# Moving additions of expert rows, and one stream's normed rows, from VectorE to GpSimd

## The chip, the cores and the metric

The kernel runs on one core of a Trainium2 chip. The metric is the time of one execution on the device in microseconds (us), the median over several runs.

## The reference

A residual x of 32 x 128 tokens with 128 features goes through four layers, each of an attention against a context of the same size and a layer of experts. In short:

```python
x = x + memory_hops(context, layernorm(x))        # first attention, two hops
x = x + top2_experts(layernorm(x))                # 8 experts, 512 hidden, gelu
x = x + linear_attention(layernorm(x), context)   # second attention, 16 heads of 8
x = x + top2_experts_gated(layernorm(x))          # 8 experts, 256 hidden
x = x + latent_attention(context, layernorm(x))   # third attention, 16 heads of 64
x = x + top2_experts_silu(layernorm(x))           # 8 experts, 256 hidden
x = x + masked_attention(layernorm(x), context)   # fourth attention, one head
x = x + top1_expert(layernorm(x))                 # 8 experts, 512 hidden
```

With two experts for a token, each expert writes its weighted output rows, and the two rows of a token are added to x at the start of the attention that follows.

## The kernel before, in words

**Layout.** x stays in SBUF as `X` (`x_rows`): 32 tiles of 128 tokens by 128 features. Four tiles are a group (`G = 4`), so there are eight groups. The second and the fourth attention run in two turns (`TURNS = 2`) of four streams (`W = 4`): group g = 4 i + w is stream w of turn i. Each stream has two PSUM banks. TensorE weaves the streams: it turns the normed rows of streams 0 to 3 (L665), then makes the queries of each, and so on.

**Expert rows.** The experts' stage before wrote two rows for each token into DRAM by indirect DMAs that GpSimd issues (L1539). `load_pairs` brings them back (SyncE, L1709): eight loads of 512 KB, the first four at once, each of the others when the same stream's load of turn 0 has landed (`pairs_here[w]`). The tile in the rows below is `paired_rows`. `combine_stream` waits for `pairs_here[w]`, and `combine` adds the two rows of a group's tokens to x in two TENSOR_TENSORs of 128 x 512 on VectorE (L566). The second attention does it for the first layer's experts, the fourth for the third layer's. In both, `next_rows` adds and then makes the statistics of a stream (`known`: L480, L476). The groups of turn 0 come first. In the second attention groups 4 to 7 are then fitted in between steps of turn 0: group 4 before the maxima, 5 before the read of the attention's output, 6 before the read of the projection, 7 after the tail's norms. In the fourth, groups 4 and 5 come right after the head's norms, 6 and 7 after the maxima.

**Norms.** `norm_rows` is used for the head of a turn (rows that go into the attention) and for its tail (rows that go to the next experts). ScalarE makes the scales by a logarithm and an exponential, `refine_scales` refines them in one step of three VectorE instructions (L449 to L451), and then four TENSOR_SCALARs of 128 x 128 for each stream subtract the mean and multiply by the scale (L498); both scalars are columns in SBUF. Each stream signals TensorE when its four are done. In the fourth attention the tail of turn 1 is made in two halves by functions of its own. There `placed_together` (L2773, L2774), behind the head's norms of turn 1, reads counts from the bank of stream 3, and TensorE turns stream 3 into that bank only after it. In the second attention L1801 adds the projection (L1859) to x; in the fourth L2746 makes the maxima of the scores (L2638), and L2755 reads the mixed rows (L2646).

**GpSimd.** It has no instructions in the second attention. In the fourth it fills a padding tile (a memset, a drain, a cast at L2606), and later sends rows to DRAM by indirect DMAs. The third attention begins on GpSimd with `norm_context`: a copy (L2058), a drain, a subtraction (L2060), a drain, a product (L2062). In the routing stages GpSimd issues indirect DMAs at L745 and L2120, in the experts' stages at L1530 and L1539. A `drain` lets what is behind it on its engine start when what is ahead of it is done.

Of the kernel before, what the change touches and what calls it, by code (L numbers as in the profile page):

```python
# [13 lines left out]
ALU = mybir.AluOpType  # L14
# [9 lines left out]
P = 128  # L24
B = 32
G = 4
NG = B // G
# [92 lines left out]
def build(nc, A, out):  # L120
    with ExitStack() as top:
# [122 lines left out]
        pairs_combined = counter("pairs_combined")  # L244
        latents_normed = counter("latents_normed")
# [200 lines left out]
        def refine_scales(ch, dve, rstd, work):  # L446
# [4 lines left out]
            ch.link(dve.scalar_tensor_tensor(rstd, sq, 1.5, rstd, ALU.add, ALU.mult))  # L451

        def scales_by_log(ch, dve, i, tail, var, rstd, work, begun=False):
# [4 lines left out]
            refine_scales(ch, dve, rstd, work)  # L458
# [29 lines left out]
        def norm_rows(dve, ch, i, tail, st, src, dst, signal, free=None, begun=False):  # L488

            if not begun:  # L490
                ch.link()
            scales_by_log(ch, dve, i, tail, st["mv"][:, :, 1], st["rstd"][:, :], st["work"], begun)
# [9 lines left out]
        def head_norms(dve, ch, i, SS, st, T, begun=False):  # L502
# [3 lines left out]
                      lambda w: dve.wait_ge(SS[w].act.sem, turn_before(SS[w].ACT, i)), begun)  # L506
# [79 lines left out]
        def tail_norms(dve, ch, i, SS, st, T, taken=False, src=x_tile):  # L586
# [5 lines left out]
            for w in range(W):  # L592
                aggregate_stream(dve, st, w)
            norm_rows(dve, ch, i, 1, st, lambda w: src(i * W + w), lambda w: tile_in(T[w]["tl"]["rows"]),
                      lambda w, ins: ins.then_inc(SS[w].dve.sem, SS[w].DVE.tick("tail_normed")))
# [1115 lines left out]
        def close_rows(layer):  # L1711
            for c in pairs_here:
                c.value += 16 * TURNS

# [18 lines left out]
        def attention_1(layer_before):  # L1733
            assert layer_before in SCATTERED
            with ExitStack() as ph:
# [28 lines left out]

                @block.vector
                def _(dve):
# [40 lines left out]
                    for i in range(TURNS):  # L1807
                        if i == 0:
                            head_norms(dve, ch, i, SS, st, T)
# [4 lines left out]
                        tail_norms(dve, ch, i, SS, st_tail, T, taken=True)  # L1814
                        for _ in ahead:
                            pass
                        if i < TURNS - 1:
                            begin_scales(dve, ch, st)
                            keep_logits(dve, i, SS, T)
                            head_norms(dve, ch, i + 1, SS, st, T, True)  # L1820
# [69 lines left out]
                close_streams(SS)  # L1890
                close_rows(layer_before)
# [667 lines left out]
        def attention_3(layer_before):  # L2559
            SCALE = float(P) ** -0.5  # L2560
            with ExitStack() as ph:
# [165 lines left out]
                def _(dve):  # L2727
# [76 lines left out]
                    for i in range(TURNS):  # L2804
                        if i == 0:
                            head_norms(dve, ch, i, SS, st, T)
# [4 lines left out]
                        if i < TURNS - 1:  # L2811
                            tail_norms(dve, ch, i, SS, st_tail, T, src=last_x)
# [4 lines left out]
                            head_norms(dve, ch, i + 1, SS, st, T, True)  # L2817
# [50 lines left out]
```

## Time and profile before

| what | us |
|---|---|
| median of 3 runs | 1673.55 (1666.23 to 1673.93) |
| the profiled execution | 1664.46 |
| its span | 1662.6 |
| second attention, about | 357 to 440 |
| fourth attention, about | 1438 to 1520 |

The span is the time from the first to the last instruction of the profiled execution; its time is 1.9 us more. TensorE's granted clock was 0.897 of full speed in the mean. In the rows, PE is TensorE, DVE VectorE, ACT ScalarE, POOL GpSimd and SPq SyncE's queue; L566 is line 566 of the kernel before. A bracket behind a row is the idle time of the engine before it and what ended it; "issue" means that the profile shows no releaser.

### The profile page before, as it was taken

The numbers are of one execution on the slowest core, as the hardware profiler recorded it, in microseconds if no ns is written. First come the engines' busy times: TensorE is split into PE (matmuls) and PEld (weight loads), VectorE is DVE, ScalarE is ACT, GpSimd is POOL, SyncE is SP. The second block draws the span as 40 slices with busy tenths as digits, with TensorE's granted clock in tenths as the row PEclk, the third lists the DMA queues.
The fourth block names the chain that finished last, engine by engine and source line by source line (L and its number), as shares of the span: only waits on it lengthen the run. The fifth ranks groups of instructions, "written<-read, shape, count | busy, mean of one in ns | idle before, by whom it ended". The sixth has DMA issues, their size and how long they took to land. (4 is left out here: it accounts for less than half of the span.)

```text
span 1662.6 us, 37562 instructions
## 1 busy us (share of the span) xinstructions
PE 1398.9 (84%) x10866; PEld 1301.8 (78%) x10867; DVE 1121.4 (67%) x3528; ACT 903.6 (54%) x2726; POOL 767.3 (46%) x775
## 2 busy tenths in 40 slices
PE   6687699946877389999999999999998399667398
PEld 4566599945666289999999999999998399545298
DVE  5646755558767367778787877878776466576455
ACT  4354155522323178777778787777775134244254
POOL 4066444420004454556757575757554456303344
PEclk9797899977657699999999999999999699878599
DMA  9201122250220300000000000000000323531322
GB/s 233 34 32 57 52 57 67 64 182 1 103 75 30 123 14 1 14 2 19 10 16 10 7 19 0 25 0 13 1 14 6 107 79 84 164 103 52 115 81 70
DMA packets 88412, 88.70 MB, mean 53 GB/s; under 512 B 17058, under 2 KB 74761, under 8 KB 87927
## 3 DMA queue, kind: packets, MB, share of 16 engines
q1 hardware_dynamic: 72472, 58.20, 12.8%
q0 software_dynamic: 12448, 26.27, 4.6%
q10 hardware_dynamic: 3392, 3.02, 0.7%
q8 instruction: 47, 0.77, 0.2%
q14 instruction: 53, 0.43, 0.1%
HBM read 54.06 MB, written 34.91 MB: 54 GB/s over the span
## 5 line engine op out<-in xcount | busy, mean ns | idle before, releaser
L2130 POOL TENSOR_TENSOR paired_rows<-paired_rows,rinv 128x1024 f32<-128x1024 f32 x128 | 242.7, 1896 | 243.6 <-DVE rinv L2451 228.6
L2442 DVE TENSOR_TENSOR probs_turned_lo<-psum_banks,probs_turned_hi 128x512 fp32r<-128x512 f32 x256 | 175.5, 686 | 137.7 <-ACT probs_turned_hi L2295 133.3
L2321 ACT ACTIVATE paired_rows<-psum_banks,neg_max 128x256 f32<-128x256 f32 x512 | 237.2, 485 | 0.6 <-DVEq L2022 0.4
L2242 PE MATMUL psum_banks<-probs_turned_hi,y_rows 128*128 128x256 f32 x1024 | 214.8, 293 | 0.9 <-DVEq L2022 0.9
L2192 PE MATMUL psum_banks<-y_turned_parts,queries_hi 128*128 128x256 f32 x1024 | 199.6, 293 | 3.0 <-DVEq L2022 3.0
L2242 PEld LDWEIGHTS psum_banks<-probs_turned_hi,y_rows 128*128 128x128 f32 x1024 | 167.5, 190 | 1.7 <-DVEq L2022 1.6
L2295 ACT CAST probs_turned_hi<-psum_banks 128x512 fp32r<-128x512 f32 x256 | 151.2, 591 | 19.9 <-PE psum_banks L2163 8.3
L2192 PEld LDWEIGHTS psum_banks<-y_turned_parts,queries_hi 128*128 128x128 f32 x1024 | 157.7, 190 | 3.6 <-issue 3.6
L2163 PE MATMUL psum_banks<-ident,paired_rows 128*128 128x128 f32 x1024 | 155.5, 274 | 5.3 <-DVE probs_turned_lo L2442 2.9
L2457 DVE TENSOR_REDUCE neg_max<-psum_banks 128x4 f32<-128x1024 f32 x128 | 155.4, 1214 | 3.7 <-PE psum_banks L2192 3.5
L2192 PE MATMUL psum_banks<-y_turned_parts,queries_lo 128*128 128x256 f32 x512 | 145.0, 283 | 0.0
L2242 PE MATMUL psum_banks<-probs_turned_lo,y_rows 128*128 128x256 f32 x512 | 144.5, 282 | 0.0
L2295 ACT CAST queries_hi<-psum_banks 128x512 fp32r<-128x512 f32 x128 | 75.0, 586 | 106.0 <-PE psum_banks L2228 97.6
L2163 PEld LDWEIGHTS psum_banks<-ident,paired_rows 128*128 128x128 f32 x1024 | 116.7, 140 | 8.7 <-DVE probs_turned_lo L2442 3.6
L1601 ACT ACTIVATE hidden<-psum_banks,tile_w 128x128 f32<-128x128 f32 x284 | 81.4, 368 | 65.4 <-PE psum_banks L1564 51.2
L1539 POOL DMA_INDIRECT expert_rows<-expert_rows_sb,tile_rows x71 | 68.1, 959 | 97.1 <-DVE expert_rows_sb L1648 94.8
L2321 ACT ACTIVATION_READ_ACCUMULATOR paired_rows<-psum_banks,neg_max 128x1 f32 x512 | 110.2, 215 | 0.0
L2228 PE MATMUL psum_banks<-y_turned_parts,wqk_hi 128*128 128x256 f32 x512 | 103.8, 295 | 0.8 <-POOL y_turned_parts L2054 0.8
L2242 PEld LDWEIGHTS psum_banks<-probs_turned_lo,y_rows 128*128 128x128 f32 x512 | 97.7, 191 | 0.0
L2192 PEld LDWEIGHTS psum_banks<-y_turned_parts,queries_lo 128*128 128x128 f32 x512 | 97.1, 190 | 0.0
L745 POOL DMA_INDIRECT rows_by_expert_first<-paired_rows,top_experts x64 | 62.5, 976 | 70.7 <-DVE mix_weights L1126 49.3
L1539 POOL DMA_INDIRECT expert_rows<-expert_rows_sb__,tile_rows x71 | 68.2, 960 | 58.1 <-ACT expert_rows_sb__ L1608 57.4
(721 smaller groups left out, 3787.1 us busy)
## 6 DMA issues: line engine op xcount, KB each, us to landing
paired_rows<-expert_rows SPq DMA_DIRECT2D x16, 512.0 KB, 6.0
expert_w_a<-rows_by_expert_last SPq DMA_DIRECT2D x39, 129.0 KB
tile_rows<-rows_by_expert_first SPq DMA_DIRECT2D x71, 65.0 KB
tile_rows<-rows_by_expert SPq DMA_DIRECT2D x71, 65.0 KB
expert_w_b<-in_L_ffn_w_dram SPq DMA_DIRECT2D x2, 2048.0 KB, 12.6
tile_rows<-expert_rows SPq DMA_DIRECT2D x8, 512.0 KB, 3.7
x_rows<-in_x_dram SPq DMA_DIRECT2D x8, 256.0 KB, 5.4
ctx_turned_dram<-ctx_turned SPq DMA_DIRECT2D x1, 2048.0 KB, 11.1
```

What stands on the lines that cost most here:

```text
L745: pool.indirect_dma_start(xfirst, bass.IndirectOffsetOnAxis(ap=first_spots[:, i, k, t:t + 1], axis=0), ROWS[:, i * N + t, :], None).then_i ...
L1539: pool.indirect_dma_start(ys, bass.IndirectOffsetOnAxis(ap=to, axis=0), yo[:, i % SLOTS, :], None).then_inc(expert_out[i % SLOTS].sem, 16)
L1601: ins = act.activation(hidT[:, s % 2, c * P:(c + 1) * P], hidden_bank(s, c // 2)[:, c % 2 * P:(c % 2 + 1) * P], ACT.Gelu, bias=w1[:, s % 4 ...
L2130: ins = pool.tensor_tensor(probs[:, k, :, :], probs[:, k, :, :], rinv[:, k, :].unsqueeze(2).to_broadcast([P, 4, 256]), ALU.mult)
L2163: ins = pe.transpose(bank[T_BANK][:, h * P:(h + 1) * P], probs[:, par, h, c * P:(c + 1) * P], ident[:, :])
L2192: ins = pe.matmul(bank[S_BANKS[par] + r][:, h * 256:(h + 1) * 256], queries[q][:, h, r, :], yparts[:, 2 * s2 + y, r * 256:(r + 1) * 256], ...
L2228: ins = pe.matmul(bank[Q_BANK][:, h * 256:(h + 1) * 256].rearrange("p (r q) -> p r q", r=2), wqk_parts[w][:, 2 * u3 + h, :], latents_of, s ...
L2242: ins = pe.matmul(bank[Z_BANK][:, r * 256:(r + 1) * 256], yrows[:, 2 * s1 + y, (2 * r + k) * P:(2 * r + k + 1) * P], probsT[x][:, (u + 1) ...
L2295: ins = act.copy(dst, bank[bank_][:, :])
L2321: ins = act.activation(probs[:, par, h, :], bank[S_BANKS[par] + h // 2][:, (h % 2) * 256:(h % 2 + 1) * 256], ACT.Exp, bias=nmax[:, par, h: ...
L2442: ins = dve.tensor_tensor(lo, bank[bank_][:, :], hi.bitcast(F32), ALU.subtract)
L2457: ins = dve.tensor_reduce(nmax[:, par, :], ps[:, S_BANKS[par]:S_BANKS[par] + 2, :].rearrange("p r (h k) -> p (r h) k", k=256), AX.X, ALU.m ...
```

## The change

In the second and the fourth attention GpSimd makes the additions of groups 2 to 7 (six of eight), with a drain between the two additions of a group, and VectorE waits for a count (`pairs_added`) instead of adding. And GpSimd makes the normed rows of stream 3: a subtraction and a product of 128 x 512 with the mean and the scale broadcast, and a drain between them, after VectorE has refined the scales (`scales_refined`, raised by the last instruction of `refine_scales`). That goes for the four norms of the second attention and for the first three of the fourth; the fourth's last tail stays as it was. GpSimd's order is: additions of groups 2 and 3, head norm, additions of groups 4 to 7, tail norm, head norm (and in the second attention a tail norm). In the fourth this stands behind the padding tile and ahead of the indirect DMAs. Cut to its core:

```diff
+        def last_stream_norm(pool, n, st, src, dst, signal, free=None):
+            own = slice((W - 1) * G, W * G)
+            pool.wait_ge(scales_refined.sem, scales_refined.value + n)
+            if free:
+                free()
+            pool.tensor_tensor(dst, src, st["mv"][:, own, 0:1].to_broadcast([P, G, P]), ALU.subtract)
+            pool.drain()
+            pool.tensor_tensor(dst, dst, st["rstd"][:, own].unsqueeze(2).to_broadcast([P, G, P]), ALU.mult).then_inc(signal, 1)
...
+        POOL_GROUPS = [g for g in range(NG) if g >= W // 2]
+
         def combine_stream(dve, ch, i, w, layer):
 
+            g = i * W + w
+            if g in POOL_GROUPS:
+                dve.wait_ge(pairs_added.sem, pairs_added.value + POOL_GROUPS.index(g) + 1)
+                return
             dve.wait_ge(pairs_here[w].sem, i * 16 + (pairs_here[w].value + 16))
-            combine(dve, ch, i * W + w, layer)
+            combine(dve, ch, g, layer)
+
+        def combine_on_pool(pool, layer, i):
+
+            for g in POOL_GROUPS:
+                if g // W != i:
+                    continue
+                w = g % W
+                pool.wait_ge(pairs_here[w].sem, i * 16 + (pairs_here[w].value + 16))
+                for k in range(CHOICES[layer]):
+                    if k:
+                        pool.drain()
+                    ins = pool.tensor_tensor(group(X, g), group(X, g), YY[:, bass.ds(g * G, G), k, :], ALU.add)
+                ins.then_inc(pairs_added.sem, 1)
...
@@ norm_rows
-            for w in range(W):
+            for w in range(W - 1 if by_pool else W):
...
@@ attention_1, a new GpSimd stream
+                @block.gpsimd
+                def _(pool):
+                    combine_on_pool(pool, layer_before, 0)
+                    for i in range(TURNS):
+                        own, S = group(X, i * W + W - 1), SS[W - 1]
+                        last_stream_norm(pool, 2 * i + 1, st, own, T[W - 1]["u"][:, :, :], S.dve.sem, lambda: pool.wait_ge(S.act.sem, turn_before(S.ACT, i)))
+                        if i < TURNS - 1:
+                            combine_on_pool(pool, layer_before, i + 1)
+                        last_stream_norm(pool, 2 * i + 2, st_tail, own, T[W - 1]["tl"]["rows"][:, :, :], S.dve.sem)
...
@@ attention_3, GpSimd, ahead of its spreads
+                    combine_on_pool(pool, layer_before, 0)
+                    S = SS[W - 1]
+                    first, second = ((i * W + W - 1) * G for i in range(TURNS))
+                    last_stream_norm(pool, 1, st, X[:, first:first + G, :], T[W - 1]["u"][:, :, :], S.dve.sem, lambda: pool.wait_ge(S.act.sem, turn_before(S.ACT, 0)))
+                    combine_on_pool(pool, layer_before, 1)
+                    last_stream_norm(pool, 2, st_tail, LAST_ROWS[:, first:first + G, P:2 * P], T[W - 1]["tl"]["rows"][:, :, :], S.dve.sem)
+                    last_stream_norm(pool, 3, st, X[:, second:second + G, :], T[W - 1]["u"][:, :, :], S.dve.sem, lambda: pool.wait_ge(S.act.sem, turn_before(S.ACT, 1)))
```

## Rows read from the trace of the kernel before

**Rows 1.** Page, part 1: busy us of each engine, share of the span, instructions.

```profile
PE 1398.9 (84%) x10866; PEld 1301.8 (78%) x10867; DVE 1121.4 (67%) x3528; ACT 903.6 (54%) x2726; POOL 767.3 (46%) x775
```

**Rows 2.** Timeline, VectorE, second attention: start, duration, line, tiles; in brackets the wait before.

```profile
367.62 1.43 DVE L566 TENSOR_TENSOR x_rows<-x_rows,paired_rows 128x512 f32<-128x512 f32 x2
...
370.47 0.38 DVE L476 BATCH_NORM_AGGREGATE mean_var__<-norm_stats__ 128x2 f32<-128x6 f32 x4
...
375.56 1.11 DVE L498 TENSOR_SCALAR u_rows___<-x_rows,mean_var__,rstd__ 128x128 f32<-128x128 f32 x4
...
403.81 0.69 DVE L1801 TENSOR_TENSOR x_rows<-x_rows,psum_banks 128x512 f32<-128x512 f32 x1 [0.98 <-PE psum_banks L1859]
```

**Rows 3.** Timeline, TensorE, second and fourth attention.

```profile
376.72 1.12 PE L665 MATMUL psum_banks<-ident,u_rows___ 128*128 128x128 f32 x4
...
1476.02 3.82 PE L2646 MATMUL psum_banks<-ctx_rows,expert_w_a 128*128 128x128 f32 x32
...
1508.26 0.63 PE L665 MATMUL psum_banks<-ident,u_rows___ 128*128 128x128 f32 x4 [0.90 <-DVE ends L2774]
```

**Rows 4.** Timeline, VectorE, fourth attention.

```profile
1468.79 0.69 DVE L2746 TENSOR_REDUCE neg_max<-psum_banks 128x4 f32<-128x512 f32 x1 [3.14 <-PE psum_banks L2638]
...
1479.14 1.13 DVE L2755 SCALAR_TENSOR_TENSOR paired_rows<-psum_banks,rinv,x_rows 128x128 f32<-128x128 f32 x4
```

**Rows 5.** Groups by form, VectorE and GpSimd: busy us, mean ns | idle before, releaser.

```profile
L566 DVE TENSOR_TENSOR x_rows<-x_rows,paired_rows 128x512 f32<-128x512 f32 x32 | 21.8, 682 | 12.5 <-DMA paired_rows<-expert_rows 10.9 <-issue 0.5
...
L2071 POOL TENSOR_TENSOR x_rows<-x_rows,paired_rows 128x512 f32 x10 | 12.9, 1295 | 2.6 <-issue 2.6
```

**Rows 6.** Timeline, GpSimd, start of the third and of the fourth attention.

```profile
558.27 0.19 POOL L2058 COPY group_scale<-ctx_rstd 128x4 f32<-128x4 f32 x1 [1.78 <-POOLq L1446]
567.71 1.04 POOL L2060 TENSOR_TENSOR context_normed<-ctx_rows,ctx_mean_var 128x512 f32<-128x512 f32 x1 [9.25 <-issue]
568.91 1.03 POOL L2062 TENSOR_TENSOR context_normed<-context_normed,group_scale 128x512 f32<-128x512 f32 x1 [0.15 <-issue]
...
1446.01 0.36 POOL L2606 CAST last_pad<-spare_row 128x1 uint32<-128x1 f32 x1 [7.26 <-issue]
```

**Rows 7.** Timeline, SyncE's DMA queue, second attention.

```profile
362.37 0.36 SPq L1709 DMA_DIRECT2D paired_rows<-expert_rows  x1
```

**Rows 8.** Page, part 5: GpSimd's indirect DMAs before attention stages.

```profile
L1539 POOL DMA_INDIRECT expert_rows<-expert_rows_sb,tile_rows x71 | 68.1, 959 | 97.1 <-DVE expert_rows_sb L1648 94.8
...
L745 POOL DMA_INDIRECT rows_by_expert_first<-paired_rows,top_experts x64 | 62.5, 976 | 70.7 <-DVE mix_weights L1126 49.3
...
L1539 POOL DMA_INDIRECT expert_rows<-expert_rows_sb__,tile_rows x71 | 68.2, 960 | 58.1 <-ACT expert_rows_sb__ L1608 57.4
```

**Rows 9.** Groups by line, GpSimd, windows 500 to 557 and 1283 to 1311 us.

```profile
L1530 POOL DMA_INDIRECT tile_rows<-normed_rows_dram,source_rows x16 | 16.0, 997 | 28.4 <-SPq L1446 23.9 <-issue 4.3 <-PE psum_banks L1554 0.3
...
L1539 POOL DMA_INDIRECT expert_rows<-expert_rows_sb_,pair_rows x16 | 15.9, 996 | 5.3 <-issue 3.7 <-ACT expert_rows_sb_ L1610 1.0 <-DMA expert_rows<-expert_rows_sb_,pair_rows 0.6
...
L2120 POOL DMA_INDIRECT rows_by_expert<-paired_rows,top_experts x16 | 15.4, 963 | 19.7 <-DVE top_experts L2408 15.4 <-issue 4.3
```

**Rows 10.** Timeline, VectorE and ScalarE, start of the third attention.

```profile
565.81 0.17 DVE L2518 TENSOR_SCALAR rows_work<-rows_mv 128x8 f32<-128x8 f32 x1
...
571.83 0.20 ACT L2279 ACTIVATE rows_work<-rows_work 128x8 f32<-128x8 f32 x1
```

**Rows 11.** Timeline, VectorE and GpSimd side by side; last a group of VectorE.

```profile
348.98 0.52 DVE L1648 TENSOR_SCALAR expert_rows_sb<-expert_rows_sb,tile_rows 128x128 f32<-128x128 f32 x1
...
348.51 0.96 POOL L1539 DMA_INDIRECT expert_rows<-expert_rows_sb,tile_rows  x1 [0.94 <-DVE expert_rows_sb L1648]
...
134.12 1.11 DVE L498 TENSOR_SCALAR u_rows__<-x_rows,mean_var_,rstd_ 128x128 f32<-128x128 f32 x4
...
135.04 0.32 POOL L750 COPY paired_rows<-mix_weights 128x4 f32<-128x4 f32 x1 [5.32 <-ACT u_turned L642]
...
L1648 DVE TENSOR_SCALAR expert_rows_sb<-expert_rows_sb,tile_rows 128x128 f32<-128x128 f32 x71 | 20.3, 286 | 0.1
```

More of the change, by code:

```diff
@@ L244, in build @@
         pairs_combined = counter("pairs_combined")
+        scales_refined = counter("scales_refined")
+        pairs_added = counter("pairs_added")
         latents_normed = counter("latents_normed")
@@ L444, in seed_scales, with refine_scales @@
             ch.link(dve.tensor_scalar(rstd.bitcast(I32), bits, -1.0, RSQRT_SEED, ALU.mult, ALU.add))
-        def refine_scales(ch, dve, rstd, work):
+        def refine_scales(ch, dve, rstd, work, refined=None):
             half, sq = work[:, 0, :], work[:, 1, :]
@@ L450, in refine_scales, with scales_by_log @@
             ch.link(dve.tensor_tensor(sq, sq, half, ALU.mult))
-            ch.link(dve.scalar_tensor_tensor(rstd, sq, 1.5, rstd, ALU.add, ALU.mult))
-        def scales_by_log(ch, dve, i, tail, var, rstd, work, begun=False):
+            ins = dve.scalar_tensor_tensor(rstd, sq, 1.5, rstd, ALU.add, ALU.mult)
+            if refined:
+                ins.then_inc(refined.sem, 1)
+            ch.link(ins)
+        def scales_by_log(ch, dve, i, tail, var, rstd, work, begun=False, refined=None):
             if not begun:
@@ L457, in scales_by_log @@
             dve.wait_ge(roots_made.sem, i * 2 + (roots_made.value + 1 + tail))
-            refine_scales(ch, dve, rstd, work)
+            refine_scales(ch, dve, rstd, work, refined)
         def roots_by_log(act, i, tail, st):
@@ L486, in known, with norm_rows @@
             aggregate_stream(dve, st, w)
-        def norm_rows(dve, ch, i, tail, st, src, dst, signal, free=None, begun=False):
+        def norm_rows(dve, ch, i, tail, st, src, dst, signal, free=None, begun=False, by_pool=None):
             if not begun:
                 ch.link()
-            scales_by_log(ch, dve, i, tail, st["mv"][:, :, 1], st["rstd"][:, :], st["work"], begun)
-            for w in range(W):
+            scales_by_log(ch, dve, i, tail, st["mv"][:, :, 1], st["rstd"][:, :], st["work"], begun, scales_refined if by_pool else None)
+            for w in range(W - 1 if by_pool else W):
                 if free:
@@ L500, in norm_rows, with head_norms @@
                 signal(w, ins)
-        def head_norms(dve, ch, i, SS, st, T, begun=False):
+            if by_pool:
+                by_pool()
+        def last_stream_norm(pool, n, st, src, dst, signal, free=None):
[6 more added lines that the diff above has]
+            pool.tensor_tensor(dst, dst, st["rstd"][:, own].unsqueeze(2).to_broadcast([P, G, P]), ALU.mult).then_inc(signal, 1)
+        def head_norms(dve, ch, i, SS, st, T, begun=False, pooled=False):
             norm_rows(dve, ch, i, 0, st, lambda w: x_tile(i * W + w), lambda w: tile_in(T[w]["u"]),
                       lambda w, ins: ins.then_inc(SS[w].dve.sem, SS[w].DVE.tick("u_normed")),
-                      lambda w: dve.wait_ge(SS[w].act.sem, turn_before(SS[w].ACT, i)), begun)
+                      lambda w: dve.wait_ge(SS[w].act.sem, turn_before(SS[w].ACT, i)), begun,
+                      (lambda: SS[W - 1].DVE.tick("u_normed")) if pooled else None)
         def begin_scales(dve, ch, st):
@@ L584, in tail_tiles, with tail_norms @@
                     "ix": sb_in(ph, "tail_index", [P, G, E], U32), "lg": sb_in(ph, "tail_logits", [P, G, E])}
-        def tail_norms(dve, ch, i, SS, st, T, taken=False, src=x_tile):
+        def tail_norms(dve, ch, i, SS, st, T, taken=False, src=x_tile, pooled=False):
             if not taken:
@@ L594, in tail_norms @@
             norm_rows(dve, ch, i, 1, st, lambda w: src(i * W + w), lambda w: tile_in(T[w]["tl"]["rows"]),
-                      lambda w, ins: ins.then_inc(SS[w].dve.sem, SS[w].DVE.tick("tail_normed")))
+                      lambda w, ins: ins.then_inc(SS[w].dve.sem, SS[w].DVE.tick("tail_normed")),
+                      by_pool=(lambda: SS[W - 1].DVE.tick("tail_normed")) if pooled else None)
         def tail_dve(dve, ch, g, i, S, tl, logits_bank, hot=None, to=ROWS.bitcast(U32)[:, :, P]):
@@ L1713, in close_rows @@
                 c.value += 16 * TURNS
+            pairs_added.value += len(POOL_GROUPS)
         def load_expert_weights(sp, layer):
@@ L1813, in _ @@
                         ch.link()
-                        tail_norms(dve, ch, i, SS, st_tail, T, taken=True)
+                        tail_norms(dve, ch, i, SS, st_tail, T, taken=True, pooled=True)
                         for _ in ahead:
@@ L1890, in attention_1 @@
                 close_streams(SS)
+                scales_refined.value += 2 * TURNS
                 close_rows(layer_before)
@@ L2805, in _ @@
                         if i == 0:
[L2806 removed]
+                            head_norms(dve, ch, i, SS, st, T, pooled=True)
                         ahead = next_rows(dve, ch, i + 1, st, here, (2, 2))
```

8 lines of the change are left out of this document (4 added, 4 removed).

## The prediction

> **What bounds the kernel now.** I read the page's totals first [rows 1]. TensorE is busy for 84% of the span, VectorE for 67% and GpSimd for 46%, so over the whole kernel VectorE isn't the limit, and GpSimd has room. But the change touches two stages, the second attention (357 to 440 us) and the fourth (1438 to 1520 us), and there the order of VectorE's work has to be read from its timeline. The reader should look at two things in it: what ends a wait, and what would be late next if VectorE were done sooner.
>
> At the start of the second attention [rows 2] each group has its additions and then its statistics, and the last of these end at 370.85. The refined scales are there at 372.40, and 16 TENSOR_SCALARs (four for each stream, one each 0.257 us) give the normed rows of streams 0 to 3 at 373.59, 374.61, 375.64 and 376.67. TensorE turns the last of these at 376.72 for 1.12 us [rows 3]: a turn takes it as long as VectorE needs for a stream, so what makes stream 2 late makes everything after it as late. Later additions are mostly put in front of waits: at 403.81 VectorE had waited 0.98 us for TensorE, at 1468.79 it had waited 3.14 us [rows 2, 4]. The groups of additions that start at once are the costly ones: of 21.8 us in 32 additions only those that start a stage, or stand ahead of something that is ready, are on the path [rows 5].
>
> **The change, part by part.** *Additions taken from VectorE.* 24 of 32 additions go, 24 x 0.682 = 16.4 us [rows 5], and 28 TENSOR_SCALARs of 0.257 = 7.2 us. If all of it lay on the path the kernel would gain 23.6 us; that is one bound. In the second attention the additions of group 4 stand behind the head's norms (0.68 us each, ahead of the waits for TensorE's first products), the others ahead of waits as that at 403.81 [rows 2]. I take -0.1. In the fourth all four groups of turn 1 stand between the maxima and the mixed rows. There TensorE's mixed products of the first stream (32 products in 3.82 us, that is four streams, 0.96 each) start at 1476.02, and VectorE reads them at 1479.14 [rows 3, 4]. Ready they were at about 1477.2 (0.96 and some 0.2 until the wait is passed): -1.9.
>
> *Additions put on GpSimd.* The same shape takes it 1.295 us [rows 5], with 0.15 us between two instructions that a drain parts [rows 6], so 2.75 us for a group. The pairs of group 2 land at 362.37, when SyncE's queue passes its wait for them and issues the seventh load [rows 7]. Without anything else groups 2 and 3 would have their rows at 362.5 + 2 x 2.75 + 0.15 = 368.1, against VectorE's 369.05 (367.62 + 1.43) [rows 2]; as VectorE has the statistics of group 2 to make in between, I count -0.65.
>
> *The drain between the two additions.* This is the term with the widest bounds. Nothing in the kernel before drains GpSimd in the second attention. Where it does drain, the trace has two kinds of gap [rows 6]. After compute alone it is 0.15 us. After a stretch of indirect DMAs it is 7.26 us in the fourth attention, between a memset and the cast at 1446.01, and 9.25 us at the start of the third, between a copy and the subtraction at 567.71, and the profile names no releaser ("issue"). The indirect DMAs since the last drain are 71 + 16 = 87 in the one case, and 64 + 71 + 16 + 16 = 167 in the other [rows 8, 9]. 7.1 / 87 = 0.082 us for each; 9.1 / 167 = 0.054, so it grows with their number, or to a limit. At the second attention 64 + 71 = 135 wait. Bounds: 7.3 us (the nearest smaller count) and 11 us (135 x 0.082), and below nothing, -0.65, if the drain's gap belongs to something else. I take 9.1. Group 2: first addition 362.5 to 363.8, drain to 372.9, second to 374.2; group 3 at 374.2 + 2.75 + 0.15 = 377.1, seen by VectorE at about 377.2. Statistics and aggregates of that stream ended 370.85, 1.8 us after its additions (369.05) [rows 2]: now 379.0. **+8.1.** VectorE stands in the wait for group 2 with everything behind it, and TensorE has nothing until the first stream is normed.
>
> *The refund.* The third attention's first drain now has only 16 + 16 = 32 indirect DMAs behind it: 32 x 0.082 = 2.6 us, and GpSimd's rows come 6.6 us earlier. What follows them is ScalarE's root at 571.83 [rows 10]. It queues behind ScalarE's work for TensorE; what VectorE made for it was there at 565.98. So 571.83 - 565.98 = 5.85, less some 0.15 between two engines: **-5.7** at most. What would be late next is VectorE's own start of that stage; bounds 0 and -5.7. I take -5.7, as TensorE waits there too. In the fourth attention the long drain is there already: GpSimd is free at 1446.37 [rows 6], and its two groups come to 1446.4 + 2 x 2.75 + 0.15 = 1452.0 while VectorE makes those of groups 0 and 1. VectorE is rid of four additions there, but has to wait for these; I estimate -0.4, somewhat over half an addition of 0.68.
>
> *The norms on GpSimd.* Seven norms of stream 3 (four in the second attention, three in the fourth) become two TENSOR_TENSORs as those at 567.71 and 568.91, 1.04 us each, and a drain [rows 6]: 2.23 us for 1.03. Alone that costs nothing: they start with stream 0 and are done before stream 2 (3.17 us). But do the two engines run beside each other? Two places say no [rows 11]. The TENSOR_SCALAR of L1648 takes 0.286 us on average; the one at 348.98 takes 0.52 and ends at 349.50, GpSimd's instruction at 349.47. And at 135.04, where VectorE makes normed rows, GpSimd's copy of 128x4 takes 0.32 us, against 0.19 at 558.27 [rows 6]; the four TENSOR_SCALARs from 134.12 on keep their pace of 0.257, and GpSimd's copy gets in behind them while VectorE's stream goes on. So both engines hold something in turn, and a short instruction waits for a long one. How often GpSimd gets in isn't shown: after each of VectorE's instructions, or every second, or only when VectorE stops. I take every second (0.26 us apart, and GpSimd has 0.15 us between two of its own). Then 12 TENSOR_SCALARs take 3.1 us plus each GpSimd instruction that falls in.
>
> Two of the seven norms (the head's of turn 0) are followed on GpSimd by the additions of groups 4 to 7. Five of its instructions fall between six pairs: 2 x 1.04 + 3 x 1.295 = 6.0. Stream 2 comes 9.0 us after the scales instead of 3.17: **+5.9 each, +11.8**. Four more have only the two instructions: +2.1 where TensorE's turns set the pace, 2.1 - 1.03 = +1.1 where VectorE's next work does (it is rid of stream 3). The mean is 1.6: **+6.4**. The seventh stands ahead of a wait of 0.90 us of TensorE for L2774 [rows 3], which is VectorE's: 2.1 - 1.03 = **+1.1**.
>
> By the Trainium skill (SBUF — State Buffer, section "Who interferes with whom") VectorE and GpSimd share one pair of ports, a tensor_scalar in a two-port mode takes it, as does an instruction with two inputs in SBUF for GpSimd's reads, and who issues first holds it for the whole instruction. The stretched instruction at 348.98 agrees; by this rule the norms pay, as in my sum, and without it they would cost nothing.
>
> **Sum:** 8.1 - 5.7 + 11.8 + 6.4 + 1.1 - 0.1 - 0.4 - 1.9 = +19.3, that is 1.2%. The profiled execution took 1664.46 us, with 1662.6 of span, so it would come to 1683.8. The median of the runs is 1673.55, 9.1 above it, and would come to 1692.9. As the runs of one kernel lie 7.7 us apart, I put the prediction a little below: 1690.
>
> **The rivals.**
> *GpSimd waits while VectorE streams.* If it only gets in when VectorE stops, streams 0 to 2 are on time, and stream 3 comes at 3.1 + 2.2 = 5.3 instead of 4.2, seven times: +7.7, less the wait of 0.9. With the rest, 8.1 - 5.7 + 6.8 - 2.4 = +6.8: 1680. The uninterrupted four TENSOR_SCALARs at 134.12 speak for it, the copies at 135.04 against. 0.2.
> *One for one.* If GpSimd gets in after each TENSOR_SCALAR, ten of its instructions fall into each of the two head norms: 2.1 + 8 x 1.295 = 12.4 each. Sum: 24.8 + 6.4 + 1.1 + 2.4 - 2.4 = +32: 1706. 0.1.
> *The drain is paid, the refund isn't.* If TensorE isn't waiting at the third attention's start, +25: 1699. 0.05.
> *On the other side: no collision.* If a TENSOR_SCALAR with two scalars out of SBUF leaves GpSimd alone, the norms cost nothing, the wait for L2774 goes (-0.9), and the sum is 8.1 - 5.7 - 2.4 - 0.9 = -0.9; if the drain doesn't stall either, -0.65 - 3.3 = -4: 1670 to 1673. It decides from the point at which a GpSimd instruction costs the stream under 0.2 us. The quiet pace at 134.12 speaks for it, 348.98 against. 0.15.
> *All of VectorE's time was on the path:* -23.6 + 2.4 (drain less refund) = -21: 1652. The waits at 403.81 and 1468.79 speak against it. 0.05; and with what the small cases leave, faster has 0.07.
>
> **How the numbers follow.** My sum has 0.45. A measurement of this kernel can tell about 0.5%, 8.4 us, from no change. Slower beyond that are my sum, the one-for-one case and the missing refund, and about a third of the case with +6.8: 0.68. Within it are the rest of that case and the case without a collision: 0.25. Faster: 0.07. The range runs from 1668 (no collision, with a low run) to 1707 (one for one); outside lie the case at 1652 and sums over several upper bounds.
>
> **What the changed profile would show.** Right: in the second attention a gap of 7 to 11 us on GpSimd between the two additions of group 2, statistics ending near 379, and at the third attention a first drain under 4 us with ScalarE's root at 566 to 567. TENSOR_SCALARs of L498 of 1 us and more wherever GpSimd has an instruction, and streams of 2 to 4 us. In the fourth attention the mixed rows read at 1.2 us after TensorE's start. Wrong: the gap is 0.15 us; or L498 keeps 0.257 us beside GpSimd's 1.05; or the third attention's root comes no sooner although the drain is short. The prediction fails most easily on how the two engines take turns, 18 of its 19 us hang on that.

## The result, and the profile after

The changed kernel is slower: the ratio of its time to the kernel before is 1.0164, with a 95% interval of 1.0138 to 1.0191. The medians are 1697.37 us (1691.28 to 1698.70, 4 runs) and 1673.74 us (1666.23 to 1674.72, 4 runs), 23.6 us apart. The ratio isn't the quotient of these two medians, which is 1.0141; by it the cost is 27 us. Measured again beside other kernels the change gave 1.0112 (1.0053 to 1.0171), so its cost is some 19 to 27 us. The prediction was 1690 with a range of 1668 to 1707, from a sum of +19.3.

The profiled execution took 1698.70 us, 34.2 more than the profiled one of before. To see where, I matched ScalarE's instructions one by one in the two traces, since ScalarE's program is the same, and read how much later each starts:

| ScalarE's instruction, line before | before, us | after, us | later by |
|---|---|---|---|
| last experts' tile before the second attention, L1601 | 341.42 | 347.10 | 5.68 |
| roots of turn 0, second attention, L463 | 371.18 | 382.56 | 11.38 |
| exponentials of a stream, behind the head norm, L1838 | 382.26 | 402.61 | 20.35 |
| late in the second experts, L1596 | 544.99 | 567.48 | 22.49 |
| third attention, past its start, L2295 | 590.05 | 609.38 | 19.33 |
| third experts, L1596 | 1401.02 | 1428.10 | 27.08 |
| roots of turn 0, fourth attention, L463 | 1454.67 | 1480.53 | 25.86 |
| stream 2 turned, L2677 | 1460.33 | 1493.43 | 33.10 |
| roots of the tail, L463 | 1488.15 | 1519.12 | 30.97 |
| tail turned, L642 | 1491.77 | 1524.23 | 32.46 |
| last experts, L1601 | 1645.29 | 1679.65 | 34.36 |

In the stages that the change touches, the differences of this column add up to 5.7 + 9.0 + 2.1 - 3.2 - 1.2 + 7.2 - 2.1 + 1.5 + 1.9 = +20.9. The other 13.4 lie in stages with the same code: 5.7 ahead of the second attention, which varies from one execution to the next (the profiles of the change and of the first eight experiments lie from -0.6 to +8.4 there), and 7.75 in the third attention and the experts behind it, which is told at the end. A second profile of the changed kernel gives +21.1 for the same stages.

The totals, for [rows 1]:

```profile
PE 1409.6 (83%) x10866; PEld 1310.8 (77%) x10867; DVE 1121.6 (66%) x3476; ACT 902.7 (53%) x2726; POOL 811.5 (48%) x813
```

VectorE lost 52 instructions and is busy for as long as before: what it was spared came back as longer instructions. The timeline of GpSimd in the second attention, changed kernel (L587 is the addition, L514 and L516 the norm):

```profile
368.26 1.48 POOL L587 TENSOR_TENSOR x_rows<-x_rows,paired_rows 128x512 f32<-128x512 f32 x1 [8.97 <-DMA paired_rows<-expert_rows]
376.70 3.88 POOL L587 TENSOR_TENSOR x_rows<-x_rows,paired_rows 128x512 f32<-128x512 f32 x3 [6.96 <-issue]
383.85 1.04 POOL L514 TENSOR_TENSOR u_rows___<-x_rows,mean_var__ 128x512 f32<-128x512 f32 x1 [3.26 <-DVE rstd__ L453]
385.03 1.09 POOL L516 TENSOR_TENSOR u_rows___<-u_rows___,rstd__ 128x512 f32<-128x512 f32 x1
386.09 10.73 POOL L587 TENSOR_TENSOR x_rows<-x_rows,paired_rows 128x512 f32<-128x512 f32 x8
```

The second row is the drain: between the two additions of group 2 nothing runs for 6.96 us, and the profile names no releaser. The same stretch on VectorE, which answers to [rows 2]:

```profile
378.00 0.87 DVE L485 BATCH_NORM_STATS2 norm_stats__<-x_rows 128x6 f32<-128x128 f32 x4 [6.30 <-POOL x_rows L587]
...
380.62 0.87 DVE L485 BATCH_NORM_STATS2 norm_stats__<-x_rows 128x6 f32<-128x128 f32 x4 [1.30 <-POOL x_rows L587]
...
383.59 0.18 DVE L453 SCALAR_TENSOR_TENSOR rstd__<-newton__,rstd__ 128x16 f32<-128x16 f32 x1
383.87 3.57 DVE L503 TENSOR_SCALAR u_rows<-x_rows,mean_var__,rstd__ 128x128 f32<-128x128 f32 x4
387.36 3.02 DVE L503 TENSOR_SCALAR u_rows_<-x_rows,mean_var__,rstd__ 128x128 f32<-128x128 f32 x4
390.29 3.96 DVE L503 TENSOR_SCALAR u_rows__<-x_rows,mean_var__,rstd__ 128x128 f32<-128x128 f32 x4
394.18 0.86 DVE L485 BATCH_NORM_STATS2 norm_stats__<-x_rows 128x6 f32<-128x128 f32 x4
```

VectorE waits 6.30 us for group 2 and 1.30 for group 3. Then four TENSOR_SCALARs take 3.57, 3.02 and 3.96 us, where they took 1.11 [rows 2]; the third stream was not done until about 394.2, when the next statistics begin. Its scales were there at 383.77, so 10.4 us for three streams instead of 3.2.

That is 7.2 of the 9.0 us between the roots and the exponentials in the table. The other 1.7 us go with TensorE's clock: two streams' projections take 1.56 us longer together. The first projections of turn 0 (kernel before, then changed kernel):

```profile
378.17 1.16 PE L1859 MATMUL psum_banks<-wsmall,u_turned 128*128 128x128 f32 x8
```

```profile
396.75 2.08 PE L1907 MATMUL psum_banks<-wsmall,u_turned 128*128 128x128 f32 x8
399.29 1.80 PE L1907 MATMUL psum_banks<-wsmall,u_turned_ 128*128 128x128 f32 x8
401.33 1.16 PE L1907 MATMUL psum_banks<-wsmall,u_turned__ 128*128 128x128 f32 x8
```

Before, the granted clock was 0.50 (1.2 GHz) from 373 to 378 us and 1.00 (2.4 GHz) from 378 to 395, when TensorE had turned four streams without a wait. In the changed kernel it waited 1.83 and 2.77 us for the streams that VectorE made late, the clock was 0.50 from 380 to 400 us and 0.98 from 400 to 414, and two streams' projections ran at the lower level.

A norm that has no additions behind it on GpSimd shows the collision by itself (VectorE, then GpSimd, turn 1 of the second attention):

```profile
436.09 2.60 DVE L503 TENSOR_SCALAR u_rows<-x_rows,mean_var___,rstd___ 128x128 f32<-128x128 f32 x4
438.61 1.10 DVE L503 TENSOR_SCALAR u_rows_<-x_rows,mean_var___,rstd___ 128x128 f32<-128x128 f32 x4
```

```profile
436.07 1.04 POOL L514 TENSOR_TENSOR u_rows___<-x_rows,mean_var___ 128x512 f32<-128x512 f32 x1 [39.26 <-DVE rstd___ L453]
437.25 1.09 POOL L516 TENSOR_TENSOR u_rows___<-u_rows___,rstd___ 128x512 f32<-128x512 f32 x1
```

While GpSimd has its two instructions, from 436.07 to 438.34, VectorE makes four TENSOR_SCALARs in 2.60 us; the four behind them take 1.10. So each such norm makes all later streams 1.5 us late. At the start of the third attention (GpSimd, then ScalarE; for [rows 6, 10]) the drain is short now:

```profile
580.73 0.18 POOL L2107 COPY group_scale<-ctx_rstd 128x4 f32<-128x4 f32 x1 [1.79 <-POOLq L1483]
584.01 1.04 POOL L2109 TENSOR_TENSOR context_normed<-ctx_rows,ctx_mean_var 128x512 f32<-128x512 f32 x1 [3.10 <-issue]
```

```profile
590.08 0.21 ACT L2328 ACTIVATE rows_work<-rows_work 128x8 f32<-128x8 f32 x1 [1.73 <-DVE rows_work L2567]
```

The gap is 3.10 us for 9.25. The root starts 590.08 - 580.73 = 9.35 us after GpSimd's first instruction, for 571.83 - 558.27 = 13.56 before; ScalarE now waits for VectorE, which is what was next. And in the fourth attention TensorE's mixed products start at 1508.93 and VectorE reads them at once, which answers to [rows 4]:

```profile
1510.11 1.13 DVE L2811 SCALAR_TENSOR_TENSOR paired_rows<-psum_banks,rinv,x_rows 128x128 f32<-128x128 f32 x4 [1.51 <-PE psum_banks L2702]
```

### The profile page after: what moved, and what is told of

The parts are those of the page before. It is cut to its first block and busy times, and to the rows that moved or that the text cites. A ratio compares the mean times of both kernels' runs of the same rounds, so it can differ in the third digit from the quotient of the medians.

```text
span 1696.9 us, 37547 instructions
## 1 busy us (share of the span) xinstructions
PE 1409.6 (83%) x10866; PEld 1310.8 (77%) x10867; DVE 1121.6 (66%) x3476; ACT 902.7 (53%) x2726; POOL 811.5 (48%) x813
## 3 DMA queue, kind: packets, MB, share of 16 engines
q10 hardware_dynamic: 3392, 3.02, 0.7%
## 6 DMA issues: line engine op xcount, KB each, us to landing
ctx_turned_dram<-ctx_turned SPq DMA_DIRECT2D x1, 2048.0 KB, 10.4
```

## The experiments

The theory at this point: the loss has two causes, a drain that pays for the indirect DMAs that GpSimd issued before it, and TENSOR_SCALARs of VectorE that take turns with GpSimd's instructions. The rival to the first is a gap that belongs to its place, the rival to the second that VectorE is only waiting for what GpSimd makes late. Ratios are to the kernel before on the same chip.

### A lone drain in the kernel before

```diff
 # attention_1, nothing else on GpSimd
+                @block.gpsimd
+                def _(pool):
+                    pool.drain()
```

> The kernel before, with one drain and nothing else on GpSimd in the second attention, where no engine waits for GpSimd. Theory (the drain pays for the indirect DMAs issued since the last drain, wherever it stands): the first drain of the third attention falls from 9.25 us to about 3.1, as in the changed kernel, the root there comes some 4 us sooner after the stage's start, and the time falls by 3.5 to 5 us, to a ratio of 0.997 to 0.998. Rival (the long gap belongs to the third attention itself): the gap stays near 9 us and the ratio is 1.000.

Measured: 0.9964 (0.9944 to 0.9985), 1663.66 against 1668.88 us. At the start of the third attention GpSimd's rows are:

```profile
559.75 0.18 POOL L2062 COPY group_scale<-ctx_rstd 128x4 f32<-128x4 f32 x1 [1.79 <-POOLq L1446]
562.71 1.04 POOL L2064 TENSOR_TENSOR context_normed<-ctx_rows,ctx_mean_var 128x512 f32<-128x512 f32 x1 [2.78 <-issue]
```

One instruction that computes nothing took 6.5 us out of a gap in another stage and made the kernel faster, by 5 us between the medians and 6 by the ratio. The gap doesn't belong to the third attention. By the matched instructions the refund is 3.6 us (from +1.44 at L1596 to -2.20 at L2295), and the interval of the ratio, 2.5 to 9.3 us, holds that. No version of the study was measurably faster than this one.

Inside the third attention the kernel before has smaller gaps of the same kind, each at a drain between a copy and a subtraction, after three and after five indirect DMAs (L2120) since the last drain:

```profile
875.65 0.74 POOL L2054 TENSOR_TENSOR y_turned_parts<-expert_w_b,y_turned_parts 128x256 fp32r<-128x256 f32 x1 [0.41 <-issue]
898.86 0.73 POOL L2054 TENSOR_TENSOR y_turned_parts<-expert_w_b,y_turned_parts 128x256 fp32r<-128x256 f32 x1 [0.92 <-issue]
```

Where no indirect DMA stands between two such drains the gap is 0.15 us.

### The additions alone, and the norms alone

```diff
 # additions alone: all normed rows on VectorE, no last_stream_norm
-    head_norms(..., pooled=True)
+    head_norms(...)
 # norms alone: VectorE adds all groups
-        POOL_GROUPS = [g for g in range(NG) if g >= W // 2]
+        POOL_GROUPS = []
```

> The change without its norms: GpSimd makes the additions of groups 2 to 7, VectorE all normed rows. Theory: the long drain at the start of the second attention stays (+5.7), the refund stays (-3.5), each head norm of turn 0 meets five or six of GpSimd's eight additions of 1.3 us (+7 each), the other norms meet nothing, the mixed rows gain 2: some +15 us, ratio 1.009. Rival (the norms on GpSimd are what costs): within 4 us of the kernel before, ratio 1.000 to 1.002.

> The change without its additions: VectorE adds all groups, GpSimd makes the normed rows of stream 3 in seven norms. Theory: the long drain now stands inside the first norm, so that stream 3 is there about 9 us after the scales instead of 4.2 (+5), the refund stays (-3.5), and seven norms with two GpSimd instructions each lose 1 to 1.5 (+8): some +9 us, ratio 1.005. Rival (the additions are what costs): 0 to +2, ratio 1.000.

Measured: 1.0108 (1.0074 to 1.0141) for the additions, 1.0030 (1.0006 to 1.0054) for the norms. Both cost, the additions more. The first rival is refuted. The second, +2 us at most, lies inside the interval of the norms (1 to 9 us), and the trace speaks against it: the matched instructions lose 7.0 us between the roots of turn 0 and the exponentials (8.61 to 15.65). GpSimd's timelines (additions alone, then norms alone) show that the long gap goes with the first drain, whichever it is:

```profile
370.50 14.50 POOL L587 TENSOR_TENSOR x_rows<-x_rows,paired_rows 128x512 f32<-128x512 f32 x11 [6.96 <-issue]
```

```profile
381.09 1.04 POOL L514 TENSOR_TENSOR u_rows___<-x_rows,mean_var__ 128x512 f32<-128x512 f32 x1 [19.01 <-DVE rstd__ L453]
389.09 1.04 POOL L516 TENSOR_TENSOR u_rows___<-u_rows___,rstd__ 128x512 f32<-128x512 f32 x1 [6.96 <-issue]
```

It is 6.96 us in both and in the change, though the drain was reached 10.5 us after the end of the last indirect DMA's instruction in the additions alone and in the change (at 363.5 and 369.7 us), and 20.0 us after it in the norms alone (at 382.1). Waiting 10 us longer doesn't shorten it, as if the work were only done when a drain asks for it. In the kernel with the additions alone two of VectorE's three refining instructions and its first stream are stretched as well:

```profile
377.60 0.66 DVE L451 TENSOR_TENSOR newton__<-rstd__ 128x16 f32<-128x16 f32 x1 [0.56 <-ACT rstd__ L470]
378.33 0.17 DVE L452 TENSOR_TENSOR newton__<-newton__ 128x16 f32<-128x16 f32 x1
378.59 1.08 DVE L453 SCALAR_TENSOR_TENSOR rstd__<-newton__,rstd__ 128x16 f32<-128x16 f32 x1
379.75 3.87 DVE L503 TENSOR_SCALAR u_rows<-x_rows,mean_var__,rstd__ 128x128 f32<-128x128 f32 x4
```

### The additions of groups 4 to 7 behind VectorE's norm

```diff
 # the same in attention_3
+                            pool.wait_ge(SS[W - 2].dve.sem, SS[W - 2].DVE.at(i, "u_normed"))
                             combine_on_pool(pool, layer_before, i + 1)
```

> The change whole, but GpSimd starts the additions of groups 4 to 7 only when VectorE has finished its streams of the head norm of turn 0 (in both attentions). Theory (VectorE's TENSOR_SCALARs and GpSimd's instructions shut each other out): both head norms lose about 2 us instead of 8, so 11 to 12 us of the change's 23 are gone: ratio 1.006 to 1.008 against the kernel before. Rival (GpSimd is only late, and VectorE waits for what it makes): additions later still, no better than the change, ratio 1.014 or more.

Measured: 1.0079 (1.0047 to 1.0111). Against the change's 1.0164 half of the loss is gone by adding a wait; against its 1.0112 when measured again it is less than a third, and the intervals overlap. The trace is clearer. VectorE's head norm of the second attention:

```profile
377.69 2.60 DVE L503 TENSOR_SCALAR u_rows<-x_rows,mean_var__,rstd__ 128x128 f32<-128x128 f32 x4
380.21 1.10 DVE L503 TENSOR_SCALAR u_rows_<-x_rows,mean_var__,rstd__ 128x128 f32<-128x128 f32 x4
```

Only the norm's two instructions collide; the third stream is turned 1.5 us late instead of 7.2, in both attentions. From the roots to the exponentials the second attention loses 1.7 us for 9.0. The rival, that the additions come too late, would have given 1.014 or more and is refuted: later is better.

### Semaphores in place of the drains

```diff
-            pool.drain()
+            # raised by the instruction before: .then_inc(own_steps.sem, 1)
+            pool.wait_ge(own_steps.sem, own_steps.value)
```

> The change whole, with the drains between GpSimd's additions and inside its norms replaced by a semaphore that the first instruction raises and GpSimd waits for. Theory (it is the drain that pays for the indirect DMAs): no gap of 7 us in the second attention (-5.7), the third attention's first drain is 9 us again (+3.5 to 5): ratio 1.013 to 1.016, as the change, but the second attention's statistics end 5 to 6 us sooner. Rival (after indirect DMAs GpSimd is slow to finish anything, drain or not): the gap stays at 7 us and the ratio at 1.016.

Measured: 1.0133 (1.0093 to 1.0172). GpSimd, second and third attention:

```profile
371.02 5.75 POOL L591 TENSOR_TENSOR x_rows<-x_rows,paired_rows 128x512 f32<-128x512 f32 x4 [8.96 <-DMA paired_rows<-expert_rows]
...
589.44 1.04 POOL L2113 TENSOR_TENSOR context_normed<-ctx_rows,ctx_mean_var 128x512 f32<-128x512 f32 x1 [9.25 <-issue]
```

Four additions in 5.75 us with no gap, and the third attention has its 9.25 again. So it is the drain itself: a semaphore orders the same two instructions without the gap, and whoever drains next pays. The rival's ratio, 1.016, isn't excluded by the interval; the rows refute it. The roots of turn 0 come 0.9 us sooner than in the kernel before (+8.43 to +7.57).

### The early drain, and both repairs

```diff
                 @block.gpsimd
                 def _(pool):
+                    pool.drain()
                     combine_on_pool(pool, layer_before, 0)
```

> The change whole, with one more drain as GpSimd's first instruction in the second attention, while the pairs are still on their way. Theory (the gap is a debt of the indirect DMAs and can be paid while nobody waits): it is over at about 367 us, before the pairs of group 2 land, the gap between the additions is 0.15 us, the refund stays: 5 to 6 us of the change's 23 are gone, ratio 1.010 to 1.013. Rival (the gap belongs to the first drain behind an addition, or to the loads in flight): no change, 1.016.

> The change whole with both repairs: the early drain, and the additions of groups 4 to 7 behind VectorE's streams of the head norms. Theory: what stays is the collision of seven norms, 1.5 us each, less the refund of 3.5 to 5 and the mixed rows: +2 to +5, ratio 1.001 to 1.003. Rival (the repairs meet in the same wait): 1.006 or more.

Measured: 1.0099 (1.0070 to 1.0129) with the drain alone, 1.0039 (1.0021 to 1.0058) with the additions behind the norms as well. GpSimd with the early drain:

```profile
363.26 5.80 POOL L587 TENSOR_TENSOR x_rows<-x_rows,paired_rows 128x512 f32<-128x512 f32 x4 [8.99 <-DMA paired_rows<-expert_rows]
...
568.55 1.04 POOL L2110 TENSOR_TENSOR context_normed<-ctx_rows,ctx_mean_var 128x512 f32<-128x512 f32 x1 [3.02 <-issue]
```

The debt is paid while the pairs are on their way, and the refund stays. In the traces the two repairs add up: with both, the roots of turn 0 come 0.8 us sooner than before for 5.7 later in the change, and the head norms lose 1.7 and 1.5 us for 9.0 and 7.2. In the ratios both together take away more than either (1.0099, 1.0079, 1.0039); how much of the change's loss that is depends on which of its two measurements it is held against. The 1.0039 was above what I expected of both (1.001 to 1.003).

### The late groups alone

```diff
-        POOL_GROUPS = [g for g in range(NG) if g >= W // 2]
+        POOL_GROUPS = [g for g in range(NG) if g >= W]
 # no norms on GpSimd; the early drain; additions behind all four streams of the head norm
+                            pool.wait_ge(SS[W - 1].dve.sem, SS[W - 1].DVE.at(i, "u_normed"))
```

> No norms on GpSimd, and the additions of groups 4 to 7 alone, in both attentions, behind all four of VectorE's streams of the head norm; the early drain stays. Theory: nothing is on the path but the refund (-3.5 to -5, as the lone drain alone gave) and up to 2 us for the mixed rows and group 4: ratio 0.995 to 0.997. Rival (GpSimd's additions still hinder VectorE's later work with two inputs in SBUF, or come too late): no better than the lone drain or worse, 0.997 to 1.002.

Measured: 0.9967 (0.9944 to 0.9990). It can't be told from the lone drain, 0.9964. Even behind the norms, 16 additions off VectorE gave nothing that the runs can show, and the trace says why. All normed rows are on time, but then VectorE waits for group 4, in both attentions:

```profile
380.14 0.87 DVE L485 BATCH_NORM_STATS2 norm_stats__<-x_rows 128x6 f32<-128x128 f32 x4 [2.79 <-POOL x_rows L587]
...
1462.37 0.87 DVE L485 BATCH_NORM_STATS2 norm_stats____<-x_rows 128x6 f32<-128x128 f32 x4 [2.79 <-POOL x_rows L587]
```

In the second attention that puts the exponentials 1.3 us later (0.68 to 1.95). In the fourth the stretch up to the tail's roots gains 1.1 (-0.56 to -1.63), of which the lone drain, with all additions on VectorE, has 0.6 too. So the part of the rival that said "or come too late" is right.

### Where VectorE's instructions lie

The profiles raised a question of their own. Between 590 and 1401 us the code is the same in all kernels, and yet this stretch is longer by 7.75 us in the change, by 7.0, 6.5, 7.3 and 7.9 in the four kernels that keep both parts, and by 1.1, 1.4, -1.2 and 2.5 in the lone drain, additions alone, norms alone and late groups. The page's part 3 has one line that goes with it, packets on a queue for instructions (before, then after):

```profile
q14 instruction: 53, 0.43, 0.1%
```

```profile
q14 instruction: 73, 0.60, 0.1%
```

It is 73 in all kernels with both parts, and 52 or 53 in the others. All 20 packets more lie in one stretch of the third attention's loop (changed kernel, DMA packets from 862 to 1180 us):

```profile
q14 instruction: 20, 0.16, 0.2%
```

The kernel before has none of that queue from 840 to 1160 us. The loop's rounds are 88 us long there. They bring five packets each, and four of these fall between 862 and 874 us, around the maxima that VectorE makes late, at 872.90. So I put 16 memsets of one column on VectorE, at the start of the second attention, where it waits for the pairs, beside the change as it is.

```diff
 # attention_1, VectorE, ahead of next_rows
+                    for k in range(16):
+                        dve.memset(T[0]["dinv"][:, 0, k:k + 1], 0.0)
```

> The changed kernel as it is, beside the two that follow. In all kernels that have both the additions and the norms on GpSimd the third attention, whose code is the same in all, runs some 7 us longer than before, and 73 packets of instructions are fetched on one queue instead of 52 or 53. Theory (where VectorE's instructions lie decides it): again 73 packets, again two-turn rounds of the third attention 1.5 us longer each, ratio 1.014 to 1.018. Rival (chance of one execution): 52 packets or no longer rounds.

> The changed kernel with 16 single-column memsets more on VectorE, at the start of the second attention, where it idles 7 us for the first pairs; they move VectorE's later instructions to where they lie without the norms on GpSimd. Theory (placement): 52 or 53 packets of instructions, no added waits of 1 us at the maxima in the third attention, 6 to 8 us faster than the changed kernel of this call: ratio 1.009 to 1.013. Rival (the longer rounds come from GpSimd's work or its code): 73 packets and the changed kernel's ratio.

> The change with both repairs (early drain, additions of groups 4 to 7 behind the head norms) and the same 16 memsets. Theory: of the 1.0039 that both repairs left, some 7 us are the placement; what remains are seven norms at 1.5 us, less refund and mixed rows: ratio 0.998 to 1.001. Rival: 1.004 as before.

Measured: 1.0112 (1.0053 to 1.0171) for the change, below the 1.014 to 1.018 expected but with an interval that holds it, 1.0134 (1.0072 to 1.0196) with 16 memsets more, without the 6 to 8 us expected, and 1.0000 (0.9975 to 1.0025) for both repairs with them, as expected. The maxima in the third attention (VectorE; the change first, then with the memsets):

```profile
961.18 1.23 DVE L2506 TENSOR_REDUCE neg_max<-psum_banks 128x4 f32<-128x1024 f32 x1 [0.92 <-PE psum_banks L2212]
```

```profile
957.71 1.22 DVE L2508 TENSOR_REDUCE neg_max<-psum_banks 128x4 f32<-128x1024 f32 x1
```

With the memsets the packets are 54 and 53 for 74 and 73, there is none from 860 to 1210 us, the four waits of 0.8 to 1.1 us, one in each round of 88 us, are gone, and in the change the stretch from 590 to 1401 us is 0.3 us shorter than in the kernel before instead of 7.85 longer. The bracket at 961.18 names TensorE, but in the round at 850 us of the kernel before VectorE is the first to fall behind: an instruction 0.4 us late, its maxima 1.6, when TensorE's products are 0.1 late.

The four rounds explain 6.1 of the 7.75 us. The last 1.3 come behind the loop, and the lone drain has 1.1 there: that goes with TensorE's granted clock, which over the stretch from 1280 to 1345 us of the kernel before is 0.737 there, 0.719 in the change, 0.714 with the lone drain, and 0.758 and 0.760 in the norms alone and the change with memsets, the two that come out shorter.

In the repaired kernel with memsets the stretch is still 4.9 longer (7.9 without them): 1.5 at its start, 2.0 near 812 us, and the clock's part at the end. Near 812 us GpSimd has a gap of 2.94 us in front of L2107, where the kernel before has 0.91; the semaphores and the late groups have one of 2.85 and 2.41 at the same instruction. What makes it I can't say.

That much the profiles show. The timed runs are split: the repaired kernel went from 1.0039 to 1.0000, the change itself shows no gain (1.0112 and 1.0134, intervals that overlap over most of their width, four runs each). The two ratios of the repaired kernel were not measured side by side, and the changed kernel alone moved by more between two such measurements (1.0164 and 1.0112). So the placement is shown in the profiled executions, and what it is worth in the median stays open.

## Why the prediction was right

The sum was +19.3; the same stages measure +20.9 by the matched instructions, and the medians are 23.6 apart. The mechanisms were the two that cost. The size of most terms was off, by -2.4 us for the drain, +2.5 for the refund, +4.4 for the head norms, -2.7 for the norms that stand alone and less for the rest, and that these nearly cancel is luck.

- **The drain, +8.1:** right in kind, measured +5.7. The gap is 6.96 us, below my lower bound of 7.3. I had taken the DMAs since the last drain as 135; at 0.082 us each the gap less 0.15 is 83 of them. The debts do add: 6.8 here and 2.6 to 3.0 in the third attention make 9.4 to 9.8, for 9.1 in one drain before. The gaps are 0.15 us after none, 0.41 after 3, 0.92 after 5, 2.8 to 3.1 after 32, 7.26 after 87 and 9.25 after 167, so the price grows with the number; but 6.96 after 135 is less than 7.26 after 87. So the number alone doesn't give it. If 32 cost 2.6 and 87 cost 7.1, the 71 of L1539 would cost some 5.8 and the 64 older ones of L745 only 1.0, by my estimate; what sets these apart wasn't tried.
- **The refund, -5.7:** the drain's gap shrank as worked out (2.6 predicted, 3.10 less 0.15 measured), but in this pair of traces only 3.2 us came back, and 3.1 to 6.2 in the experiments that have it. I had named VectorE's own start as the next to be late, and it was: ScalarE's root waits 1.73 us for it.
- **The two head norms, +11.8:** measured 9.0 + 7.2 = 16.2, the term most undersized. 14.4 of it are streams that come late, 1.7 go with TensorE's lower clock, which the prediction didn't have at all. I had one of GpSimd's instructions for every two TENSOR_SCALARs, five in a head norm. All eight up to 394 us fell in: the 12 TENSOR_SCALARs took 10.3 us, with 1.5 of them for each of GpSimd's instructions. By their single times, where a drain parts two of GpSimd's instructions VectorE gets two in, where none does it gets one. The truth lies between my case and the one-for-one rival.
- **The other norms, +6.4 and +1.1:** measured +1.5 each where one stands alone (436.09, and the fourth attention's tail), for my 1.6. In the second attention the three together are hidden in part: +2.1 for +4.7 with what lies between. The last, +1.1, is +1.9 in the table, but the lone drain has +4.0 between the same two marks with nothing changed. Marks nearer to the norm (L2674 at 1503.07 and L2684 at 1516.41 of the kernel before) give +2.0 for the change, +1.9 in its second profile, +0.6 with the norms alone, and 0.1 or less in the lone drain and the additions alone.
- **The mixed rows, -1.9:** VectorE reads them 1.18 us after TensorE's start for 3.12 before, 1.9 sooner, as worked out. The table has -2.1, but the lone drain and the norms alone, which keep these additions on VectorE, have -0.6 and -0.9 there, so not all of it comes from the change. **The fourth attention's start, -0.4:** -1.2 here, -0.6 in the second profile of the change and -0.1 with the additions alone, so it can't be told. **The second attention's additions, -0.1:** nothing that shows.
- **The rival on the other side**, no collision: refuted by the 2.60 us, and by the kernels that lack a part. *GpSimd waits while VectorE streams*: refuted by the same row; both advance in turns.

By the Trainium skill (SBUF — State Buffer, "Who interferes with whom"), issue order decides who blocks, for the length of one instruction. The traces agree: the first TENSOR_SCALAR at 383.87 came 0.02 us behind GpSimd's and waited for it, and in the additions alone the tiny L453 took 1.08 us behind an addition of 1.3, for 0.18 in the change.

What the prediction missed altogether is the 7.75 us in the unchanged code of the third attention and the experts behind it. With them the profiled execution loses 28.7 us from the second attention on, where the prediction had 19.3; the medians, 23.6 apart, and the width of the range hide that.

## What to carry to other kernels

In these kernels work on GpSimd stretched VectorE's TENSOR_SCALARs (1.11 us for four became 2.6 to 4.0) but not its statistics (0.87 us for four at 378.11 of the kernel before, 0.86 beside an addition at 394.18 of the change): check what VectorE does in the same microseconds, and if it streams TENSOR_SCALARs on the path, start GpSimd's work behind them, unless VectorE then waits for it. A drain on GpSimd after 32 or more indirect DMAs cost 2.8 to 9.25 us here: put one where nobody waits for GpSimd, or order with a semaphore. Before taking additions off a busy engine, look at whether they stand ahead of a wait; 24 of them, 16 us of busy time, were worth some 2 us here.

## What the runs showed of the hardware that I had not expected

A lone drain in an idle stretch made the kernel 0.36% faster (0.15 to 0.56), since the debt of the indirect DMAs doesn't shrink by itself: 6.96 us whether the drain was reached 10.5 or 20.0 us after the last of them. The gap is 6.96 us in all five kernels that have it in the second attention. And the place of VectorE's instructions shows in a loop that wasn't touched: 20 packets of instructions more, five in each of four rounds, and in each round a wait of 0.8 to 1.1 us at the same instruction, 6.1 us in all in the profiled execution of the change; 16 memsets took it away there. Whose instructions that queue brings the profile doesn't say; that it is VectorE's is argued from the cure, and from VectorE being the first to be late.
